# Mask and maximum of the first layer's scores: eight fused VectorE instructions per step in place of two

## The reference, cut to what matters

```python
scores = jnp.einsum('bkgld,bksd->bkgls', q, k) * scale
scores = scores + encoder_attention_mask[:, :, None, :, :]
attn = jax.nn.softmax(scores, axis=-1)
out = jnp.einsum('bkgls,bksd->bkgld', attn, v)
```

## Time and profile before

| | |
|---|---|
| median of 3 runs | 2572.05 us (2567.9 to 2572.64) |
| the profiled execution, its own time | 2574.21 us |
| its span, first to last instruction | 2572.4 us |
| outside the span | 1.8 us |
| busy share of the span: PE, DVE, ACT, POOL | 94%, 49%, 33%, 31% |
| first layer, first half | about 40 to 180 us |
| first layer, second half | about 1320 to 1460 us |

### The profile page before, as it was taken

How to read it: one execution, slowest core, us unless ns; L and a number is a source line. 1 busy time by engine, 2 the same in 40 slices (tenths; PEclk the granted TensorE clock), 3 DMA queues, 4 the chain that set the end, 5 groups by cost and what they waited for, 6 DMA issues and landing times.

```text
span 2572.4 us, 40587 instructions
## 1 busy us (share of the span) xinstructions
PE 2414.6 (94%) x14896; PEld 2063.9 (80%) x14896; DVE 1257.4 (49%) x2046; ACT 856.6 (33%) x2472; POOL 795.4 (31%) x520
## 2 busy tenths in 40 slices
PE   6877999999999999999978689999999999999999
PEld 5656888888788888777766578888887888887777
DVE  6875333334533333465579753333345333434654
ACT  5863222222422222332258632222224222223221
POOL 4862322223422223220058533222234222322100
PEclk9988999999999999999989889999999999999999
DMA  4001111101010111011130021011121001110110
GB/s 179 10 10 70 42 49 49 41 33 62 33 50 33 38 35 41 29 42 57 66 145 10 13 71 53 33 49 41 39 72 34 34 33 41 41 49 13 58 41 33
DMA packets 34545, 120.16 MB, mean 47 GB/s; under 512 B 3456, under 2 KB 3712, under 8 KB 33408
## 3 DMA queue, kind: packets, MB, share of 16 engines
q1 hardware_dynamic: 34432, 118.69, 13.0%
HBM read 114.48 MB, written 4.19 MB: 46 GB/s over the span
## 4 chain that ended last, share of the span: by engine, by line
PE 83%; DVE 6%; ACT 4%; issue 4%; POOL 2%; DMA 1%; SPq 0%; DVEq 0%; ACTq 0%; POOLq 0%
PE PS L474 70%; PE PS L675 4%; PE PS L657 4%; PE PS L666 2%; PE PS L542 1%; DVE XN L1163 1%; ACT PS L967 1%; ACT AT L967 1%; DVE X L1187 1%; DMA BO<-in_bo_rows 0%; POOL XN L357 0%; DVE BNS L1197 0%; DVE X L1231 0%; DVE X L1233 0%; DVE SUM L1173 0%
## 5 line engine op out<-in xcount | busy, mean ns | idle before, releaser
L474 PE MATMUL PS<-AT,W 128*128 128x512 f32 x2496 | 602.6, 393 | 8.6 <-DVE X L1187 7.8
L474 PEld LDWEIGHTS PS<-AT,W 128*128 128x128 f32 x2496 | 470.9, 189 | 109.9 <-DVE X L1187 8.6
L1187 DVE TENSOR_TENSOR X<-PS,X 128x512 f32<-128x512 f32 x416 | 286.6, 689 | 327.6 <-PE PS L474 316.0
L474 PE MATMUL PS<-CT,W 128*128 128x512 f32 x1584 | 402.9, 404 | 31.9 <-DVE W L324 25.0
L394 POOL TENSOR_TENSOR PR<-PR,RC 128x512 f32<-128x512 f32 x128 | 133.3, 1041 | 927.2 <-DVE RC L1324 927.2
L474 PE MATMUL PS<-W,CX 128*128 128x512 f32 x1632 | 406.7, 403 | 11.3 <-DVE X L1187 6.3
L474 PE MATMUL PS<-W,CT 128*128 128x256 f32 (+1 forms) x3264 | 406.2, 284 | 0.0
L474 PEld LDWEIGHTS PS<-W,CT 128*128 128x128 f32 x3264 | 394.7, 192 | 0.8
L474 PEld LDWEIGHTS PS<-W,CX 128*128 128x128 f32 x1632 | 302.3, 190 | 84.0 <-DVE X L1187 10.6
L474 PEld LDWEIGHTS PS<-CT,W 128*128 128x128 f32 x1584 | 292.3, 191 | 91.4 <-DVE W L324 25.4
L1000 ACT ACTIVATE CX<-PS,VEC 128x512 fp32r<-128x512 f32 x128 | 88.0, 688 | 685.8 <-PE PS L675 685.8
(11 more groups left out here) (107 smaller groups left out, 2450.1 us busy)
## 6 DMA issues: line engine op xcount, KB each, us to landing
RAW<-in_wq SPq DMA_DIRECT2D x44, 512.0 KB, 4.4
RAW<-in_wo SPq DMA_DIRECT2D x44, 512.0 KB, 3.2
RAW<-in_wk SPq DMA_DIRECT2D x40, 512.0 KB, 3.2
RAW<-in_wv SPq DMA_DIRECT2D x40, 512.0 KB, 3.7
X<-in_x SPq DMA_DIRECT2D x2, 2048.0 KB, 9.0
BVR<-in_bv_rows SPq DMA_DIRECT2D x8, 512.0 KB, 3.6
BIASVR<-in_biasv_rows SPq DMA_DIRECT2D x8, 512.0 KB, 5.0
out<-X SPq DMA_DIRECT2D x4, 1024.0 KB, 4.2
```

Of the source, the lines that this page charges most:

```text
L474: ins = nc.tensor.matmul(out, lhs(c, a), rhs(c, b), start=(k == 0), stop=(k == total - 1))
L1187: V_.tensor_tensor(X[:, tile, :], PS[:, bank, :], X[:, tile, :], ALU.add).then_inc(done, 1)
```

## The change

`soft0` no longer runs one addition and one reduction over all eight heads. It runs one fused instruction per head, over 128 columns: it adds mask and scores, multiplies by -1, writes the negated scores to the buffer, and folds them with `min` from 3e38 on, so that `MX` gets the same negated maximum as before. `max0` is now posted after head 4, and `z0` after head 7. The wait of VectorE on its own `z0` goes away. ScalarE's exponentials get `scale=-1.0`, and GpSimd subtracts in place of adding, and waits for `z0` in place of `max0`.

```diff
                 def sub(s):
 
-                    pool.wait_ge(max0, hf * STEPS0 + (s + 1))
+                    pool.wait_ge(z0, hf * STEPS0 + (s + 1))
                     z = P0[s % BUFS0].rearrange("p (h t) -> p h t", t=P)[:, OWN:KV0, :]
                     nc.gpsimd.tensor_tensor(z, z, MX[:, s % BUFS0, OWN:KV0].unsqueeze(2).to_broadcast([P, KV0 - OWN, P]),
-                                            ALU.add).then_inc(sub0, 1)
+                                            ALU.subtract).then_inc(sub0, 1)
...
                         nc.scalar.activation(P0[s % BUFS0][:, h * P:(h + 1) * P], P0[s % BUFS0][:, h * P:(h + 1) * P], ACT.Exp,
-                                             bias=MX[:, s % BUFS0, h:h + 1], accum_out=SUM0[:, s % 2, h:h + 1])
+                                             bias=MX[:, s % BUFS0, h:h + 1], scale=-1.0, accum_out=SUM0[:, s % 2, h:h + 1])
                     act.wait_ge(sub0, s0 + (s + 1))
-                    nc.scalar.activation(P0[s % BUFS0][:, OWN * P:KV0 * P], P0[s % BUFS0][:, OWN * P:KV0 * P], ACT.Exp).then_inc(exp0, 1)
+                    nc.scalar.activation(P0[s % BUFS0][:, OWN * P:KV0 * P], P0[s % BUFS0][:, OWN * P:KV0 * P], ACT.Exp, scale=-1.0).then_inc(exp0, 1)
...
                     dve.wait_ge(s0_ps, s0 + (s + 1))
                     if s >= BUFS0:
                         dve.wait_ge(t0_ps, s0 + (s - BUFS0 + 1))
-                    V_.tensor_tensor(P0[s % BUFS0].rearrange("p (i e t) -> p i e t", e=2, t=P),
-                                     PS[:, B0:B0 + 4, 0:256].rearrange("p i (e t) -> p i e t", t=P),
-                                     BIASVR[:, tile * P:(tile + 1) * P].unsqueeze(1).unsqueeze(1).to_broadcast([P, 4, 2, P]),
-                                     ALU.add).then_inc(z0, 1)
-                    dve.wait_ge(z0, s0 + (s + 1))
-                    V_.tensor_reduce(MX[:, s % BUFS0, :], P0[s % BUFS0].rearrange("p (h t) -> p h t", t=P),
-                                     AXX, ALU.max, negate=True).then_inc(max0, 1)
+                    take_wait(dve)
+                    for h in range(KV0):
+                        ins = V_.tensor_tensor_reduce(P0[s % BUFS0][:, h * P:(h + 1) * P], PS[:, B0 + h // 2, h % 2 * P:(h % 2 + 1) * P],
+                                                      BIASVR[:, tile * P:(tile + 1) * P], -1.0, 3e38, ALU.add, ALU.min,
+                                                      MX[:, s % BUFS0, h:h + 1])
+                        if h == OWN - 1:
+                            ins.then_inc(max0, 1)
+                    ins.then_inc(z0, 1)
```

## The result

| | median us (runs) | ratio to before, 95% interval | profiled execution, us (span) |
|---|---|---|---|
| before | 2570.10 (20) | 1 | 2574.21 (2572.4) |
| the change | 2574.40 (20) | 1.0016 [1.0009, 1.0022] | 2572.70 (2570.8) |

The change is slower by 4 us, 0.16%: inside the band of 0.2% that the prediction called "same", and with 20 runs on each side still told from zero. So the forecast, 2574.0, met the time, but of the difference (+4.3) it had only half. The profiled execution of before was slower than any of its 20 runs (2567.5 to 2572.7), that of the change lay in its faster half. So these two traces don't show the loss in their spans, and serve to read single places.

A forecast was written before the change was run, and what follows sets the result against it. VectorE was taken to set the 3.82 us steady row step, TensorE close at 3.61. Per half +1.7 at the start and -1.0 steady gave +1.4 for both, made +2: 2574.0 against 2572.05 us; range 2566 to 2600.

The forecast's parts named there:

- The price of the short instruction: On VectorE, the instruction writing each head's column of MX adds 0.08 us, making a block 2.16 us.
- The fused one: On VectorE, one fused instruction over 128 columns takes 0.19 us from start to start.
- The rival of the held instruction: On VectorE, each short instruction waits for its fused one: block 3.0 us, +26 us, 2598 us; chance 0.38.
- The band that the prediction gave for the block: VectorE's eight fused and eight short instructions of a step take 2.16 to 2.3 us.
- the sign it gave for steps without a row addition: The forecast is wrong if these steps change by more than 0.2 us.
- The start of a half, +1.7: First steps of each half: scores wait for the later z0, delaying the query projection and GpSimd; +1.7 us per half.
- In the steady part it costs nothing: Late z0 in steady steps: TensorE reaches the scores after the release anyway, hidden by 0.1 us; cost 0.
- The steady gain, -1.0 per half: Ten row steps per half save 0.2 us each up to TensorE's 3.61, part waited away at boundaries; -1.0 us.
- The third rival: GpSimd and the chains hide everything, time stays 2572 us; chance 0.45 together with the forecast.
- The second, the full saving of 10 us: Each of 21 steps per half gains 0.24 us as ScalarE's early start shortens boundary chains; 2562 us, chance 0.17.

The follow-up runs named there:

- a2: The kernel before, with TensorE's scores of the next step waiting for max0 in place of z0, old pair kept; 2580.74 us, ratio 1.0039.
- c2: The changed kernel with the old pair (addition, early release, maximum) in step 28 of each half alone; 2569.50 us, ratio 0.9998.
- b3: The kernel before, with VectorE's row addition moved ahead of the CX and Q lows; 2559.48 us, ratio 0.9960.
- b2: The changed kernel, with VectorE's row addition moved ahead of the CX and Q lows; 2552.75 us, ratio 0.9931.
- c4: The changed kernel with the old pair in steps 0 to 4 and 28 and VectorE's row addition ahead of CX and Q; 2548.29 us, ratio 0.9914.
- a3: The kernel before, with the maximum taken over only the first 64 of each head's 128 columns; 2561.82 us, ratio 0.9965.
- c3: The changed kernel, with ScalarE waiting for z0 after all eight heads in place of max0 after five; 2572.68 us, ratio 1.0009.

## Why the prediction was right and wrong

**The price of the short instruction** was the mis-sized term. Forecast 0.08 us of VectorE each, measured 0 from start to start. The fused one was near (0.21 against 0.19), so the block is 1.70 and not 2.16. The estimate was taken from short instructions that follow one another, and from a pitch on ScalarE; VectorE's accumulator read is beside its successor. The figure that the Trainium skill gives in "Vector Engine (DVE) Microarchitecture Reference", section 5.2, would have made the block 2.27 with all 16 instructions counted; no run agrees with that. Counted for the eight fused ones alone the same figures give 8 x 0.075 + 1.07 = 1.67 by estimate, and the trace, with 1.70, agrees. The rival of the held instruction, to which 0.38 was given, and which set the upper end of the range, fell with the first rows of the trace. The band that the prediction gave for the block, 2.16 to 2.3, was missed, and so was the sign it gave for steps without a row addition: step 28 went from 3.21 to 2.70 and 3.09, steps with a Q instruction from 3.88 to 3.30, more than the 0.2 allowed.

**The start of a half, +1.7** was wrong. The loop of block, scores, block is there (2.67 where it was 2.39, scores behind a wait for the block's end), but with 1.70 in place of 2.24 it costs 0.28 once instead of 0.60. By step 4 it has gained back what it lost (block to block 11.74 and 11.47 us after the first, 11.96 and 11.97 in before), and the pair put back in these steps alone changed nothing (2574.42 for 2574.40). The mechanism costs when the release comes at 2.4 us, as the old pair with late release showed (a2: 4.3 a half).

**"In the steady part it costs nothing"** was the step that failed. It was argued from one step, where TensorE arrives later than the release. At step 28 TensorE arrives early (no projection stands in its queue since 140.95), VectorE late, and TensorE waits 1.88 us for the block's end; the next groups are slower. c2 puts this at 4.9 us, the size of the loss. The wait of before at this step, 1.22 us for the mask addition, stands in its trace, and the prediction doesn't use it:

```profile
160.95 0.62 PE L530 MATMUL PS<-KZ,Q 32*128 32x256 f32 x12 [1.22 <-DVE XN L1163]
```

With the forecast's block the release would come at 2.24, so 1.02 later than the pair's 1.22, in both halves: 2 us of the answer, to be had from one row.

**The steady gain, -1.0 per half** was right about its bound, TensorE's 3.60 for 3.82, and about the boundary wait taking the rest (CX 6.8 to 12.9 us). It missed that a projection behind the same gap of 1.94 now takes 4.6 in place of 3.04, 1.55 us each, three times in each of its profiled executions. Why the clock falls there isn't shown. Gap, matmuls and place are equal, and the TensorE work before them is closer together (3.60 a step for 3.82), but that doesn't decide it either: in the change itself the projection at 101.86 stands behind steps of 3.60 and takes 3.03, and in a2 the slow one at 143.50 stands behind steps of 3.8, the one at 109.94 behind steps of 3.60 and 3.67, and it takes 3.00.

**The clock as a whole.** The mean granted clock over the runs was 0.9736 with the change, where before had 0.977 to 0.978 (in the runs beside the experiments). In the runs of the change, of one and the same program, a mean clock lower by 0.001 goes with 1.3 to 1.6 us more. By that slope the lower clock is worth 4 to 6 us, the whole difference and perhaps more. This is a correlation, and doesn't say what makes what.

**Where the loss stands.** The first layers of both halves together (first reciprocal to last) take 274.5 and 273.1 us in the two traces of before, 274.4 and 275.1 in those of the change. So about 1 us of the 4.3 is seen in the layer, and where the rest falls can't be told: outside it, executions of one kernel differ by 3.8 us. The experiments do show there: c2 has 270.3, b3 262.6, b2 257.3, c4 253.1, a3 268.8 and a2 286.8.

**What stands.** The time (2574.4 for 2574.0) and "no change beyond 0.2%" were right partly by luck, since errors offset each other: a block too dear by 0.46, a start too dear, against a step 28 and boundaries not counted. The edits of sign and of GpSimd's semaphore were not run alone; `max0` early is worth nothing (c3). The third rival, that chains hide all, is nearest to what the traces show on VectorE. The second, the full saving of 10 us, appears once the release and the order are mended: c4 (2548.29) is 11 us under b3 (2559.48), which has the new order and the old pair.

## What to carry to other kernels

When several instructions over a shared buffer are fused, ask first when the buffer is released, and look up every step in which the other engine is there early, not a typical one: one such step in 32 was worth 4.9 us here, as much as the loss. A faster engine that only waits longer at a fixed point shows that its queue's order is the next thing to change: an instruction that others wait for doesn't belong behind one that waits. Measure the pair "order and fusion" together, since fusion was worth +4.3 us in one order and -6.7 in the other.

## What the runs showed that was not expected

- The accumulator read of a fused VectorE instruction (0.08 us) overlaps the next fused instruction entirely: a block has 0.21 us per 128 columns with both outputs.
- TensorE's twelve matmuls of 128x512 take 3.0 to 3.1 or 4.6 us behind the same idle time of 1.94 us: 0 of 4 slow in both profiles of before, 3 of 4 in both of the change, 4 of 4 in a3. What decides between the two isn't shown.
- Times of one program with spans 11 us apart line up with its mean granted clock (0.972 to 0.978).
- Putting one step in 32 back moves 4.9 us. In the traces its two gaps on TensorE shrink by 1.3 us together, and the groups behind them by 3.0: the gap is paid more than once.
